# Rotary queries of a latent attention: 64 features through full-precision products in column tiles, in place of an absorbed matrix

## The reference, cut to what matters

```python
q_hk = (hidden_q @ Wq.T).reshape(Bv, Sv, H, K)              # Wq (2048, 512)
q_big = jnp.einsum('bshk,hkq->bshq', q_hk, w_kc_q)          # (16, 128, 384)
q_big = _apply_rope(q_big, sin_q[None, :, None, :], cos_q[None, :, None, :])
kv_r = _apply_rope(kv_c, sin_k[None], cos_k[None])
q_r = jnp.einsum('bshq,hqr->bhsr', q_big, W_qr)             # (16, 384, 64)
k_r = jnp.einsum('bld,hdr->bhlr', kv_r, W_kr)               # (16, 128, 64)
scores = jnp.einsum('bhsr,bhlr->bhsl', q_r, k_r)
attn = jax.nn.softmax(scores, axis=-1)
ctx_c = jnp.einsum('bhsl,bld->bhsd', attn, kv_r)
```

## Time and profile before

| | |
|---|---|
| median of 3 runs | 1370.16 us (1369.95 to 1370.22) |
| profiled execution: its span, first to last instruction | 1368.6 us |
| around the span (median less span) | 1.56 us |
| PE busy | 98% |
| DVE busy | 70% |
| ACT busy | 46% |
| POOL busy | 50% |
| mean granted clock of PE | 0.999 |

### The profile page before, as it was taken

How to read it: one execution, slowest core, us unless ns; L and a number is a source line. 1 busy time by engine, 2 the same in 40 slices (tenths; PEclk the granted TensorE clock), 3 DMA queues, 4 the chain that set the end, 5 groups by cost and what they waited for, 6 DMA issues and landing times.

```text
span 1368.6 us, 23258 instructions
## 1 busy us (share of the span) xinstructions
PE 1338.7 (98%) x8743; PEld 1115.8 (82%) x8743; DVE 961.4 (70%) x1475; ACT 628.4 (46%) x1309; POOL 681.6 (50%) x480
## 2 busy tenths in 40 slices
PE   7999999999999999899999999999999999999998
PEld 5677778778877777799999999999878888767886
DVE  5456776659669999677777778777546777564555
ACT  3524343253333334566666666666324546631000
POOL 3342577768747775431431431500464666535663
PEclk9999999999999999999999999999999999999999
DMA  4121233323232321000000001000231222312231
GB/s 152 52 72 48 62 85 98 87 77 93 85 129 93 92 85 55 18 26 26 1 25 25 0 25 37 20 1 1 64 105 62 79 74 66 93 44 88 97 95 62
DMA packets 30883, 85.55 MB, mean 63 GB/s; under 512 B 3408, under 2 KB 3536, under 8 KB 30544
## 3 DMA queue, kind: packets, MB, share of 16 engines
q1 hardware_dynamic: 30800, 84.43, 20.2%
HBM read 83.37 MB, written 1.05 MB: 62 GB/s over the span
## 4 chain that ended last, share of the span: by engine, by line
PE 90%; DVE 5%; ACT 3%; issue 1%; DMA 0%; POOL 0%; SPq 0%; ACTq 0%; DVEq 0%; POOLq 0%
PE psum L910 25%; PE psum L911 24%; PE psum L912 24%; PE psum L1464 6%; PE psum L938 1%; PE psum L980 1%; PE psum L985 1%; PE psum L981 1%; PE psum L1372 1%; PE psum L949 1%; PE psum L1665 1%; DVE xc L2243 1%; PE psum L1639 1%; PE psum L1652 1%; PE psum L1145 1%
## 5 line engine op out<-in xcount | busy, mean ns | idle before, releaser
L660 POOL TENSOR_SCALAR wpair<-landing 128x1024 fp32r<-128x1024 f32 (+3 forms) x116 | 108.1, 932 | 370.0 <-PE psum L912 221.5
L663 POOL TENSOR_TENSOR wpair<-landing,wpair 128x1024 fp32r<-128x1024 f32 (+3 forms) x116 | 237.6, 2048 | 9.7
L910 PE MATMUL psum<-xn,wpair 128*128 128x512 f32 x548 | 220.3, 402 | 1.2 <-POOL wpair L663 1.2
L911 PE MATMUL psum<-xn,wpair 128*128 128x512 f32 x548 | 216.1, 394 | 0.0
L912 PE MATMUL psum<-xn,wpair 128*128 128x512 f32 x548 | 215.3, 393 | 0.0
L2236 DVE TENSOR_TENSOR expo_t<-psum,expo_t 128x512 fp32r<-128x512 f32 (+1 forms) x224 | 144.5, 651 | 74.3 <-ACT expo_t L2019 70.6
L2019 ACT CAST expo_t<-psum 128x512 fp32r<-128x512 f32 (+1 forms) x224 | 124.3, 565 | 115.6 <-PE psum L1464 115.6
L910 PE MATMUL psum<-expo_t,kv_pair 128*128 128x256 f32 (+1 forms) x416 | 133.6, 321 | 0.2 <-DVE expo_t L2236 0.2
L1464 PE MATMUL psum<-const,expo 128*128 128x128 f32 (+1 forms) x832 | 127.5, 273 | 1.0 <-DVE expo_t L2236 0.6
L910 PEld LDWEIGHTS psum<-xn,wpair 128*128 128x128 f32 x548 | 102.9, 188 | 27.9 <-issue 2.0
L766 POOL TENSOR_TENSOR wpair<-landing,wpair 128x512 fp32r<-128x512 f32 x80 | 121.0, 1512 | 6.7
(11 more groups left out here) (332 smaller groups left out, 3198.8 us busy)
## 6 DMA issues: line engine op xcount, KB each, us to landing
landing<-in_weights SPq DMA_DIRECT2D x75, 512.0 KB, 3.6
landing<-in_weights SPq DMA_DIRECT2D x105, 256.0 KB, 2.6
kv<-in_ctx SPq DMA_DIRECT2D x8, 832.0 KB, 4.5
landing<-in_weights SPq DMA_DIRECT2D x15, 320.0 KB, 2.9
rope_k<-in_rope_k SPq DMA_DIRECT2D x1, 1664.0 KB, 7.5
const<-in_constants SPq DMA_DIRECT2D x1, 1184.0 KB, 8.9
x<-in_x SPq DMA_DIRECT2D x4, 256.0 KB, 4.2
out<-x SPq DMA_DIRECT2D x1, 1024.0 KB, 4.2
```

What stands on the lines that cost most here:

```text
L660: pool.tensor_scalar(wpair[:, slot, 0, 0:width], landing[:, slot, 0:width], 1.0, 1.0, ALU.mult, ALU.mult).then_inc(chunk_high, 1)
L663: pool.tensor_tensor(wpair[:, slot, 1, 0:width], landing[:, slot, 0:width], wpair[:, slot, 0, 0:width].bitcast(F32), ALU.subtract).then_in ...
L910: pe.matmul(out, w(0), act(0), start=start, stop=False)
L911: pe.matmul(out, w(0), act(1), start=False, stop=False)
```

## The change

The absorbed matrix and the turned fourth tile are gone. Per head, PE now does: three query products (chunk of 384 columns); the product with W_qr, 64 rows of output, as full-precision fp32 matmuls that aren't split in three: feature tile 0 into PSUM partitions 0 to 63, tile 1 into 64 to 127, and tile 2 with its first half of the tokens into the one and the other half of the tokens into the other; four products for the states of head h + 2 (chunk of 512 columns); and one full-precision product with W_kr^T stacked twice, which adds the two halves. ACT moves the third tile's halves of 64 features to each other's partitions (`moved_halves`), which the turned tile did before, and copies the 64-feature result (`rotary_queries_in`). DVE writes the cosine products to SBUF (`turned`) and adds there. POOL does sine and addition of the third tile (`last_tile_rotated`), between its two splits. The rotary weights, 1280 bytes a partition and head, are loaded by SP without a split, 14 heads ahead of the tables, the last two later.

```diff
-    plan += [("D1", (half, CHUNK), 1), ("D1", (half, CHUNK), XH - 2), ("D1", (half, half, half), 1),
+    plan += [("D1", (half, half), 1), ("D1", (XQ, half), XH - 2), ("D1", (XQ, XQ), 1),
...
+            by_sin, shift, rotary_q = xc, xc[:, QT, :], rstd
+            turned = sb("turned", [P, 2, QT, T], F32, scope)
+            rotary_w = sb("rotary_w", [P, ROTARY_HEADS, QT * XR + P], F32, scope)
...
                     sp.wait_ge(x_ready, 4 * 3)
+                    load_rotary(0, 0, 2)
+                    load_rotary(1, 2, ROTARY_HEADS)
                     sp.dma_start(rope_k[:, :, :, :], rope_k_in.rearrange("a p k d -> p a k d")).then_inc(tables_in, 16)
                     sp.dma_start(kv[:, :, :], ctx_in[0]).then_inc(ctx_loaded, 16)
+                    for head in range(1, 6):
+                        run_region(sp, (stage, n0 + 2 * head, at0 + head * P * sum(widths), widths, 1), load)
+                    sp.wait_ge(q_lat, XH - ROTARY_HEADS)
+                    load_rotary(2, ROTARY_HEADS, XH)
...
+            def last_tile_rotated(h):
...
+                pool.wait_ge(q_halves_moved, 2 * h + 2)
+                if h:
+                    pool.wait_ge(last_rotated, h)
+                pool.tensor_tensor(by_batch(by_sin[:, 2, :]), by_batch(shift), over_batches(sin), ALU.mult
+                                   ).then_inc(last_by_sin, 1)
+                pool.wait_ge(last_by_sin, h + 1)
+                pool.wait_ge(q_by_cos, 2 * h + 2)
+                pool.tensor_tensor(turned[:, h % 2, 2, :], turned[:, h % 2, 2, :], by_sin[:, 2, :], ALU.add
+                                   ).then_inc(last_rotated, 1)
...
+                elif reps == 1:
+                    split(n0, n0 // 2, at0, n0 % 2, XQ)
+                    last_tile_rotated(XH - 3)
+                    split(n0 + 1, (n0 + 1) // 2, at0, (n0 + 1) % 2, XQ)
+                    last_tile_rotated(XH - 2)
+                    last_tile_rotated(XH - 1)
...
+                        split(n, n // 2, at0, n % 2, XQ)
+                        if head:
+                            last_tile_rotated(head - 1)
+                        split(n + 1, (n + 1) // 2, at0, (n + 1) % 2, CHUNK // 2)
...
-                def absorbed_queries(h):
...
+                def rotary_queries(h, k_bank=4):
...
+                    pe.wait_ge(q_rotated, 2 * h + 2)
+                    pe.wait_ge(last_rotated, h + 1)
+                    for side in range(2):
+                        pe.matmul(bank(k_bank)[side * XR:(side + 1) * XR, :], rotary_w[:, slot, side * XR:(side + 1) * XR],
+                                  turned[:, h % 2, side, :], start=True, stop=False)
+                    for side in range(2):
+                        mm = pe.matmul(bank(k_bank)[side * XR:(side + 1) * XR, HALVES[side]],
+                                       rotary_w[:, slot, 2 * XR:3 * XR], turned[:, h % 2, 2, HALVES[side]],
+                                       start=False, stop=True)
+                    mm.then_inc(q_rotary, 1)
+
+                def latent_queries(h, k_bank=7):
+
+                    pe.wait_ge(q_rotary_in, h + 1)
...
+                    pe.matmul(bank(k_bank), rotary_w[:, h % ROTARY_HEADS, QT * XR:QT * XR + P], rotary_q[:, :],
+                              start=True, stop=True).then_inc(q_lat, 1)
...
                     if h:
-                        absorbed_queries(h - 1)
+                        rotary_queries(h - 1)
                     if h < XH - 2:
                         head_states(h + 2)
-                    if h < XH - 1:
-                        head_absorb(h + 1)
+                    if h:
+                        latent_queries(h - 1)
...
                 score_row(0, 0, 0)
-                pe.wait_ge(rope_low, 2 * XH - 1)
+                pe.wait_ge(q_by_cos, 2 * XH - 1)
                 score_row(0, 0, 1, range(2))
-                absorbed_queries(XH - 1)
+                pe.wait_ge(q_lat_in, XH)
+                rotary_queries(XH - 1, 7)
+                latent_queries(XH - 1, 3)
...
+                def moved_halves(h):
+                    act.wait_ge(chunk_used, query_chunk(h) + 1)
+                    if h:
+                        act.wait_ge(last_by_sin, h)
+                    for to in range(2):
+                        act.copy(shift[to * XR:(to + 1) * XR, :], bank(3)[(1 - to) * XR:(2 - to) * XR, :]
+                                 ).then_inc(q_halves_moved, 1)
+
+                def rotary_queries_in(h):
+                    act.wait_ge(q_rotary, h + 1)
+                    if h:
+                        act.wait_ge(q_lat, h)
+                    act.copy(rotary_q[:, :], bank(4 if h < XH - 1 else 7)).then_inc(q_rotary_in, 1)
...
                 for h in range(XH):
-                    absorb_lows(h)
                     pair_by_sin(h)
                     pair_by_cos(h)
                     rotated(h, 0)
                     rotated(h, 1)
-                    last_by_sin(h)
                     last_by_cos(h)
-                    pair_low(h)
-                    rotated(h, 2)
                     if h < XH - 2:
                         states_low(h + 2)
-                    last_low(h)
```

More of the change, by code:

```diff
@@ L43 @@
 QT = XQ // P
+ROTARY_HEADS = 14
 KT = 13
@@ L219, in lay_out @@
     wq = i["L1_xattn_Wq"].T
-    own, turned = query_order()
+    own = query_order()
     states = lambda h: [tile(wq, k, h) for k in range(FT)]
-    absorbs = lambda h: [rows(i["L1_xattn_W_kr"][h].T), rows(i["L1_xattn_W_qr"][h].T[:, own])]
     chunk(*states(0))
-    chunk(*states(1), *absorbs(0))
+    chunk(*states(1))
     for h in range(XH):
-        kc = i["L1_xattn_w_kc_q"][h]
-        chunk(kc[:, own], kc[:, turned])
+        chunk(i["L1_xattn_w_kc_q"][h][:, own])
         if h < XH - 2:
-            chunk(*states(h + 2), *absorbs(h + 1))
-        elif h < XH - 1:
-            chunk(*absorbs(h + 1))
+            chunk(*states(h + 2))
+    to_rotary = i["L1_xattn_W_qr"][:, own, :].reshape(XH, QT, P, XR).transpose(0, 2, 1, 3).reshape(XH, P, QT * XR)
+    back = i["L1_xattn_W_kr"].transpose(0, 2, 1)
+    rotary = np.concatenate([to_rotary, np.concatenate([back, back], axis=1)], axis=2).transpose(1, 0, 2)
     wo = i["L1_xattn_Wo"].T
@@ L613, in load, with load_rotary @@
                              ).then_inc(chunk_in[slot], 16)
+            def load_rotary(part, first, end):
+                at = first % ROTARY_HEADS
+                sp.dma_start(rotary_w[:, at:at + end - first, :], rotary_in_dram[:, first:end, :]
+                             ).then_inc(rotary_loaded[part], 16)
             for region in REGIONS:
@@ L863, in c_chunks, with query_chunk @@
             return sw, down
+        def query_chunk(h):
+            return DB + 2 + 2 * h if h < XH - 1 else DB + 2 * XH - 1
         def turned_batch(i, k, last):
@@ L1340, in head_states @@
                 def head_states(h):
-                    n = DB + max(2 * h - 1, 0)
+                    n = DB + 2 * h - 1
                     chunk_ready(n)
[L1344 to L1355, removed]
-                        mm = product(bank(4)[:, k * P:(k + 1) * P],
-                                     lambda part, k=k: weight(n % 2, part, first + 1 + k, XR),
-                                     lambda part: weight(n % 2, part, first, XR), start=True, stop=True)
-                    mm.then_inc(chunk_used, 1)
+                    pe.wait_ge(hk_low, h)
+                    wide(n % 2, 0, xn, bank(0)).then_inc(chunk_used, 1)
                 def turn_keys(b, part, k_bank):
@@ L2641, in _ @@
+                    dve.wait_ge(q_by_sin, h + 1)
+                    tile = turned[:, h % 2, k, :]
+                    dve.tensor_tensor(tile, tile, by_sin[:, 1 - k, :], ALU.add).then_inc(q_rotated, 1)
                 states_low(0)
@@ L2989 @@
     arrays = lay_out({name: np.asarray(a) for name, a in inputs.items()})
-    order = ("x", "ctx_first", "ctx", "weights", "small", "constants", "rope_k")
+    order = ("x", "ctx_first", "ctx", "weights", "small", "constants", "rope_k", "rotary")
     args = [nc.dram_tensor(f"in_{name}", arrays[name].shape, F32, kind="ExternalInput").ap() for name in order]
```

136 lines of the change are left out of this document (54 added, 82 removed).

## The result

The changed kernel takes **1383.23 us** (median of 4 runs, 1380.31 to 1384.37) where the kernel before takes 1370.19 (1369.95 to 1371.29) on the same chip: ratio **1.0088** [1.0074, 1.0102]. It is slower by 13 us; 1361.1 was predicted, with a range that ended at 1369. The profiled execution took 1384.37 us, its span is 1382.6, against 1368.6 before.

What follows compares the result with a forecast made beforehand. PE bounded the kernel before, and GpSimd was to bound the changed heads; opening -3.7, heads -10.8, end +3.9 and clock +1.5 sum to -9.1 us, taking 1370.2 to 1361.1 us. Range 1353 to 1369 us.

Steps and rivals of the forecast that it cites:

- Opening: Up to head 2's first query product: absorb products and split waits go, head 2 starts earlier; 3.7 us saved (bounds 1 and 5).
- Twelve heads: Heads 2 to 13: GpSimd becomes the limit with 97.5 us, 0.5 a head of it contention, against 108.3; 10.8 us saved.
- TensorE: Its own products in heads 2 to 13, column tiles overlapping: 7.35 us a head, alone saving 1.67 a head.
- VectorE's additions: Two a head, both reading two SBUF tiles, stretched beside GpSimd's work: near 1.1 us each, not 0.69.
- End: Head 14's first query product to first scores: GpSimd's last sine and addition precede the keys' lower halves; 3.9 us lost.
- Clock: At the first scores, behind a 6 us hole in PE: clock falls to 1.2 GHz; 1.5 us lost (bounds 0 and 4).
- 1: Rival in the twelve heads: GpSimd is not slowed, 91.5 us, 6 more saved, 1355.1 us in all; chance 0.2.
- 3: Rival in the heads: column tiles run one after the other, PE 8.65 us a head, 1370.0 us in all; chance 0.06.
- 2: Rival in the heads: shared access slows GpSimd by 1.6 a head, 1374.3 us; decides from 1.26 a head; chance 0.13.
- 4: Rival: the clock falls within heads at PE's 0.8 us pauses; a few 14 us heads make it 1385; chance 0.05.
- a pitch set by TensorE: Sign against the forecast in the heads: 7.4 us throughout, instead of near 8.1 with a context step and 7.4 without.
- pairs that don't overlap: Sign against the forecast: the 64-row products' records in the heads were expected in pairs a few ns apart.

Runs made afterwards that it cites:

- e1: The changed kernel with 80 more TensorE instructions (160 satisfied waits) ahead of the first scores: 1367.85 us.
- e2: The changed kernel with 20 more TensorE instructions (40 satisfied waits) ahead of the first scores: 1368.23 us.
- e11: The changed kernel, unpadded, with the third tile's addition on VectorE and low parts of first keys and first queries formed earlier on GpSimd: 1364.13 us.
- e6: e2 with the third tile's addition done by VectorE instead of GpSimd, the sine staying on GpSimd: 1356.76 us.
- e5: e2 with the four low parts of the first keys formed earlier on GpSimd, in its stands in the last two heads: 1363.18 us.
- e7: e2 with the third tile's sine and addition both on VectorE, behind the low part of the states of head h + 2: 1377.05 us.
- e4: The kernel before with 120 more TensorE instructions (240 satisfied waits) ahead of the first scores: 1387.2 us.
- e12: The kernel before with 80 more TensorE instructions (160 satisfied waits) ahead of the first scores: 1383.52 us.

## Why the prediction was wrong

**The step that failed** is in the first paragraph: "The change touches one stage", and the sum then held only this stage; the code behind it was put at nothing without a reason. The change also took 351 instructions out of TensorE's stream, and that moved an untouched loop behind it over a block bound. No term, rival or bound had it. It is worth 15 us (e1 and e2 against the changed kernel; 13.9 in e11), of which 1 to 2.5 may be the late fall of the clock, which kernels without the stands have too. That is the sign of the result. Without it the changed kernel takes 1367.85 or 1368.23 us, inside the range, but only 3.2 to 3.5 us (0.23 to 0.25%) below the kernel before, where 9.1 (0.7%) were forecast. So the sum for the stage was mis-sized as well, above all the twelve heads.

The stage's own terms, forecast and measured (with the block shift repaired, e2; the unpadded kernel in brackets):

- **Opening** -3.7: -3.6 (-2.3, with the clock at half for 3.4 us from 415 us on). Right.
- **Twelve heads** -10.8: -6.5 (-7.2). The bound was the right one (GpSimd; e6 shows it), and the size was off. The sum of 97.5 us held 1.8 of hand-overs (0.15 a head), so 95.7 busy; measured are 97.58 busy and 3.48 idle, 101.06. So the miss of 3.6 us is half contention and half gaps: 75 to 85 ns stand before each second operation of a pair, three a head, 2.9 us in all. Nor did the contention lie where I put it: sine and addition ran nearly undisturbed (1.325 and 1.288), while the one-input pass over 384 columns took 878 ns for an estimated 520 (12 x 0.36 = 4.3 us) and the context steps 19.9 us for 17.1. Per head, gaps and contention together are (101.06 - 91.5)/12 = 0.80, not 0.5. Head pitch was 7.4 to 9.1 us, where 7.4 and 8.1 were named.
- **TensorE** 7.35 us a head: with GpSimd's load lowered it runs at 7.5 (89.95/12), with context heads in it, and 7.41 in the plain ones. The column tiles overlap as estimated: four 512-wide records in 1.08 us and four half-wide ones in 0.63, in pairs.
- **VectorE's additions**: 1428 ns at the mean where "near 1.1" was expected; the forecast's own line for failure was 1.5. VectorE was never the bound.
- **End** +3.9: +5.3. The first scores waited 6.95 us for GpSimd's last key part ("a hole of about 6 us"). In e5 the 4.2 us of it that were order went.
- **Clock** +1.5: +2.4 (scores to turned sums 20.0 for 17.57; +1.5 in the unpadded kernel).

Of the rivals, 1 and 3 did not come; 2's mechanism is there at 0.8 a head, below its turning point of 1.26; 4 came only in e7. The three signs of being wrong that the prediction ends on were a pitch set by TensorE, additions past 1.5 us and pairs that don't overlap; none of them was it.

## What to carry to other kernels

When an edit changes the number of instructions ahead of a long loop of the same engine, count where its body lies before and after (in blocks of 256 instructions, by what fits the kernels here), and look in the profile after for instruction transfers inside the loop and for waits on "issue" at its back edge; a handful of satisfied waits placed in a stand of that engine, here 20 instructions at 0.07 to 0.08 us each, can be worth 14 us. "issue" alone is no sure sign: in e4 and e12 the loss at the back edge was booked to another engine. Don't size a bound engine by its busy sum alone: add the gaps. When work moves between engines, look first at what it is queued behind: the same two operations, on one side or the other of a wait, made 1377 or 1351 us.

## What was not expected of the hardware

- A loop body of 1654 instructions runs without refetching when it lies in 7 blocks of 16 KB, and is refetched in each iteration when in 8 (8 or 9 against 25 or 26 transfers between 560 and 900 us). The bounds of blocks are offset against the built stream's start by an amount that six kernels put at 23 to 42 instructions.
- The stand at the back edge is 4.4 to 5.0 us, and with the half clock behind it a back edge costs 6.3 and 6.2 us in the changed kernel. At other positions of the body it cost 2.0 to 4.5 (e12, e4).
- A satisfied wait instruction costs TensorE 0.07 to 0.08 us (5.24 us for 80, 9.62 for 120).
- GpSimd's one-input pass, not only its two-input operations, is stretched while VectorE adds two SBUF tiles: over 384 columns it took 0.94 to 0.96 us in the ten heads of the changed kernel in which such an addition ran beside it, and 0.51 or 0.52 in two, at 472.7 us with VectorE idle and at 519.9 with VectorE multiplying out of PSUM.
